# A four-layer transformer mix on one core: the feed-forward pipeline in a new order, and the recurrence's x terms as f16 hi/lo products

## The reference

```python
x = x + rnn(layernorm(x), cond, ctx)      # per sample and step:
#   logits = concat(x_t, h) @ W_attn.T + b_attn ;  aw = softmax(logits) ;  applied = aw @ enc
#   comb = relu(concat(x_t, applied) @ W_comb.T + b_comb)
#   h = tanh(comb @ W_ih.T + b_ih + h @ W_hh.T + b_hh) ;  out_t = h @ W_out.T + b_out
x = x + moe(layernorm(x))                 # 64 experts of width 64, router, one shared expert
x = x + attention_block(layernorm(x), cond, ctx)
#   self-attention, cross-attention (16 heads), then the gated feed-forward:
#   h3 = layernorm(y) * (1 + scale) + shift ;  u = h3 @ w1 + b1 ;  a, gate = split(u)
#   y = a * gelu(gate) @ w2 + b2 + y
x = x + layernorm(x) @ W_eff              # last layer, W_eff folds weight and disha
```

## Time and profile before

| | us |
|---|---|
| median of 3 runs | 1099.95 (1096.5 to 1100.71) |
| the profiled execution | 1102.3 |
| its span, first to last instruction | 1100.6 |

### The profile page before, as it was taken

One profiled execution on the slowest core, in us unless ns is written; L12 is line 12 of the kernel. 1 busy time (PEld: TensorE's weight loads), 2 busy tenths in 40 slices (PEclk: granted clock), 3 DMA queues, 4 the chain that ended last, 5 costly groups with the idle time before them and its releaser, 6 DMA issues. The chain is left out here.

```text
span 1100.6 us, 29712 instructions
## 1 busy us (share of the span) xinstructions
PE 960.0 (87%) x12346; PEld 644.8 (59%) x12346; DVE 721.7 (66%) x1778; ACT 478.0 (43%) x889; POOL 564.9 (51%) x519
## 2 busy tenths in 40 slices
PE   3698987699999999999979968889999999898765
PEld 2476766455555555555434426677777777776443
DVE  5545445557676766677776656778787878777543
ACT  2232223132232323332322216677777777778531
POOL 4688601033433334343645554666666676667663
PEclk9555555589999999999999988999999999999877
DMA  9120024232222222312334410000000000000000
GB/s 249 32 70 1 1 49 91 48 82 78 58 78 63 77 60 77 83 59 66 108 82 114 121 52 1 2 3 3 3 3 3 3 3 3 3 3 2 3 10 29
DMA packets 46202, 51.66 MB, mean 47 GB/s; under 512 B 22101, under 2 KB 36726, under 8 KB 46070
## 3 DMA queue, kind: packets, MB, share of 16 engines
q1 hardware_dynamic: 43152, 48.78, 17.1%
q10 hardware_dynamic: 2918, 1.01, 0.5%
HBM read 48.20 MB, written 1.57 MB: 45 GB/s over the span
## 5 line engine op out<-in xcount | busy, mean ns | idle before, releaser
L706 POOL TENSOR_TENSOR ex<-ex,xn 128x512 f32<-128x512 f32 x128 | 162.7, 1271 | 276.0 <-ACT thcb L941 152.6
L941 ACT ACTIVATE thcb<-ps 128x512 f32<-128x512 f32 x132 | 79.0, 599 | 214.7 <-PE ps L1735 213.7
L787 POOL TENSOR_TENSOR wu<-encC,wu 128x1024 f16<-128x1024 f32 x64 | 137.8, 2169 | 57.6 <-ACT encC L1009 57.6
L1742 PE MATMUL ps<-ex,wd 128*128 128x512 f32 x256 | 138.9, 625 | 0.5 <-DVE xT L1360 0.5
L1348 DVE SCALAR_TENSOR_TENSOR ex<-thcb,ps 128x512 f32<-128x512 f32 x132 | 90.5, 686 | 63.5 <-ACT thcb L941 60.9
L1735 PE MATMUL ps<-xnT,wg 128*128 128x512 f16 x384 | 106.7, 388 | 3.5 <-DVE ex L1354 3.5
L1735 PE MATMUL ps<-xnT,wu 128*128 128x512 f16 x384 | 106.5, 387 | 0.0
L1682 PEld LDWEIGHTS ps<-eb,encC 128*128 128x128 f16 x3072 | 86.8, 99 | 32.3 <-DVE eb L1220 19.3
L1791 PE MATMUL ps<-wg,M 128*128 128x128 f16 x1536 | 97.7, 221 | 2.1 <-DVE wg L1438 2.1
L781 POOL TENSOR_TENSOR wd<-wd,a_sum 128x512 f32<-128x512 f32 x64 | 66.6, 1044 | 63.3 <-DVE a_sum L1469 63.3
L1002 ACT CAST wu<-ps 128x1024 f16<-128x1024 f32 x64 | 64.9, 1014 | 73.6 <-PE ps L1826 73.6
(11 more groups left out here) (300 smaller groups left out, 1807.5 us busy)
## 6 DMA issues: line engine op xcount, KB each, us to landing
xn<-coef_rows SPq DMA_DIRECT2D x128, 256.0 KB, 3.9
thcb<-in_L_ffn_Wg SPq DMA_DIRECT2D x8, 256.0 KB, 4.1
thcb<-in_L_ffn_Wu SPq DMA_DIRECT2D x8, 256.0 KB, 3.4
wd<-in_L_ffn_Wd SPq DMA_DIRECT2D x2, 1024.0 KB, 10.3
xtok<-in_x SPq DMA_DIRECT2D x4, 256.0 KB, 6.1
thcb<-in_ctx SPq DMA_DIRECT2D x2, 512.0 KB, 11.4
wu<-in_L_xcond_attn_wq SPq DMA_DIRECT2D x2, 512.0 KB, 11.1
wu<-in_L_xcond_attn_wk SPq DMA_DIRECT2D x2, 512.0 KB, 10.7
```

Source lines behind the costliest of these rows:

```text
L706: nc.gpsimd.tensor_tensor(hid[:, side(m, n), :], gu[:, side(m, n), :], other, ALU.mult)\
L787: nc.gpsimd.tensor_tensor(z[:, 1, 8 * u:8 * u + 8, :], a_Zc[:, u], z[:, 0, 8 * u:8 * u + 8, :], ALU.subtract)\
L941: nc.scalar.activation(th[:, side(m, n), :], bank(side(m, n)), ACT.Tanh, scale=0.5 / WSCALE)\
L1742: mm(bank(5), wd[:, n, :] if n < PAIRS else swd[:, :], hid[:, side(m, n), :], start=(n == 0), stop=(n == UNITS - 1)).then_inc(s["y_ready"], 1)
```

## The change

**1. x terms and biases of the recurrence.** `x_parts` and the bias of `project` are made from f16 halves. A value is split into a high and a low f16 part; a product of two split values is three products (high by high, high by low, low by high), one of ones with a split row is two. `x_parts` is now 3 + 3 + 2 f16 products of 128 columns instead of three f32 ones; the bias of `project` two f16 products instead of one in f32. ACT makes the high parts of two weights, the bias rows and ones (four copies behind the first three groups of the set-up); DVE makes three low parts ahead of the low parts of the encoder; `xnT` is split as well, high parts by ACT and low parts by DVE, four groups of 512 columns behind the encoder's. PE waits for all of them before the first step.

```diff
 def x_parts(t):
-    xs, x_bank = xnT[:, t * B:(t + TL) * B], bank(X_BANK)
-    mm(x_bank[:, 0:TL * B], w_T[:, 0, :], xs, start=True, stop=False, skip_group_check=True)
-    mm(x_bank[:, LOGITS], xs, w_attnT[:, 0, :], start=False, stop=False, skip_group_check=True)
-    mm(x_bank[:, LOGITS], ones_row[:, :], battn_row[:, :], start=False, stop=False, skip_group_check=True)
+    if t == 0:
+        pe.wait_ge(s["wx_lo"], 3)
+    for i, (u, v) in enumerate(HALVES):
+        mm(x_bank[:, 0:TL * B], wx[:, 0, u, :], xs[v], start=(i == 0), stop=False, skip_group_check=True)
+    for u, v in HALVES:
+        mm(x_bank[:, LOGITS], xs[v], wx[:, 1, u, :], start=False, stop=False, skip_group_check=True)
+    for v in range(2):
+        mm(x_bank[:, LOGITS], ones16[:, :], rows16[:, v, 0:2 * L], start=False, stop=False, skip_group_check=True)
...
+dve.wait_ge(s["wx_hi"], 4)
+for i, w in enumerate((w_T, w_attnT)):
+    V.tensor_tensor(wx[:, i, 1, :], w[:, 0, :], wx[:, i, 0, :], sub).then_inc(s["wx_lo"], 1)
+V.tensor_tensor(rows16[:, 1, :], b_rows[:, :], rows16[:, 0, :], sub).then_inc(s["wx_lo"], 1)
```

```diff
 for n in range(ITEMS):                      # POOL
     Z_low(n, 0)
     Z_low(n, 1)
-    if n >= ITEMS - 2:
-        f_rstd1(n - (ITEMS - 2))
+    if n == ITEMS - 3:
+        f_rstd1(0)
...
     normalise(n, 0)
     normalise(n, 1)
...
+    if n == ITEMS - 2:
+        f_hi_lo(0)
+    if n == ITEMS - 1:
+        f_rstd1(1)
+    if n >= ITEMS - 4 and n < ITEMS - 1:
+        f_x3_sum(n - (ITEMS - 4))
```

```diff
 for u in range(FF + FF_LAG):                # PE
     k, c = divmod(u, FC)
-    if u < FF:
+    if 0 < u < FF:
         f_up(u)
-    if u == 0:
+    if u == 1:
         PT(ITEMS - 1, 0)
         PT(ITEMS - 1, 1)
-    elif u == 1:
+    if u >= FF_LAG:
+        f_down(u - FF_LAG)
+    if u == 2:
         O(ITEMS - 1, 0)
         O(ITEMS - 1, 1)
-    elif u == 2:
+    elif u == 3:
         pe.wait_ge(s["a_OT"], ITEMS)
         back(len(STAGES) - 1)
-    if u >= FF_LAG:
-        f_down(u - FF_LAG)
-    if c == 3 and k >= 1:
-        f_n2T_(k - 1)
-    if c == 0 and k + 1 < CH:
-        f_nT(k + 1)
+    if u + 1 in F_NT:                       # F_NT = {2: 1, 5: 2, 9: 3}
+        f_nT(F_NT[u + 1])
     if c == 0 and k >= 2:
+        f_n2T_(k - 2)
+    if c == 1 and k >= 2:
         f_last(k - 2)
...
 for u in range(FF + FF_LAG):                # POOL
     k, c = divmod(u, FC)
+    if c == 2 and 1 <= k < CH:
+        f_rstd2(k - 1)
     if u < FF:
         f_hid_low(u)
+    if u in F_NT:
+        f_hi_lo(F_NT[u])
     if c == 0 and k + 2 < CH:
         f_rstd1(k + 2)
-    if c == 2 and k >= 1:
-        f_rstd2(k - 1)
-    if c == 2 and k + 1 < CH:
-        f_hi_lo(k + 1)
-    if c == 3 and k < CH:
-        f_x3_sum(k)
+    if u == FC + 2:
+        f_x3_sum(CH - 1)
...
 for u in range(FF + FF_LAG):                # ACT
-    if c == 0 and k >= 2:
+    if c == 1 and k >= 2:
         f_n2T_in(k - 2)
...
     if u < FF:
         f_hid_hi(u)
-    if c == 2 and k + 1 < CH:
-        f_h_hi(k + 1)
+    if u == 0:
+        f_norm1(1)
+    if u in F_NT:
+        f_h_hi(F_NT[u])
     if c == 2 and k + 2 < CH:
         f_norm1(k + 2)
```

More of the change, by code:

```diff
@@ L239, in build @@
         f_hs = [xT_f[:, (2 + i) * CT:(3 + i) * CT].bitcast(F16).rearrange("p (x n) -> p x n", x=2) for i in range(2)]
-        f_x3 = [tiles(xnT[:, 1024 + i * CT:1024 + (i + 1) * CT]) for i in range(2)]
+        f_x3 = [tiles(ctxT[:, k * CT:(k + 1) * CT]) for k in range(CH)]
         f_split = [(w1[:, i * CT:(i + 1) * CT], [w1h[:, x, i * CT:(i + 1) * CT] for x in range(2)]) for i in range(2)]
@@ L256, in build @@
         LAST_BANK = 7
+        F_NT = {FC * (k - 1) + 1 if k > 1 else 2: k for k in range(1, CH)}
         def f_tok(t, k):
@@ L378, in build @@
             groups.append(("xn_ready", [(i * P, tr(xn[:, 4 * g + i, :])) for i in range(4)],
-                           xnT[:, g * 512:(g + 1) * 512], None))
+                           tuple(xnT[:, g * 512:(g + 1) * 512].bitcast(F16).rearrange("p (x a b) -> p x a b", x=2, b=P)[:, x]
+                                 for x in range(2)), None))
         N_RNN = len(groups)
@@ L893, in setup @@
                     evac(act, copy, g)
-            for g in range(N_RNN):
+            for g in range(3):
+                setup(g)
+            evacuated(act, 1)
+            for i, w in enumerate((w_T, w_attnT)):
+                copy(wx[:, i, 0, :], w[:, 0, :]).then_inc(s["wx_hi"], 1)
+            act.wait_ge(s["rnn_w_in"], 16 * RNN_DMAS)
+            act.wait_ge(s["consts_ready"], 2)
+            copy(rows16[:, 0, :], b_rows[:, :]).then_inc(s["wx_hi"], 1)
+            copy(ones16[:, :], ones_row[:, :]).then_inc(s["wx_hi"], 1)
+            for g in range(3, N_RNN):
                 setup(g)
@@ L1501, in f_stats1, with f_scale @@
                 f_stats(1, k, f_tok(a2tok, k), "f_stats1")
-            def f_modulate(k):
-                scale, shift = (ss[:, i, 8 * k:8 * k + 8].unsqueeze(2).broadcast_to([P, 8, T]) for i in (4, 5))
+            def f_scale(k):
+                scale = ss[:, 4, 8 * k:8 * k + 8].unsqueeze(2).broadcast_to([P, 8, T])
                 n8, h8 = (v.rearrange("p (b t) -> p b t", t=T) for v in (bank(nT_bank(k)), f_h32))
```

102 lines of the change are left out of this document (63 added, 39 removed).

## The result

The changed kernel takes **1084.65 us** (median of four runs, 1080.55 to 1087.7); the kernel before took 1098.86 (four runs, 1096.5 to 1100.71) in the same comparison. The ratio is 0.987, with a 95% interval of 0.983 to 0.991. So the change is a gain of 14 us, clear of the spread. But it is half of the 29 us forecast, and the time lies outside the range of 1063 to 1082: 13.7 us above the 1071 forecast.

What follows compares the result with a forecast made beforehand. PE was taken to bound the recurrence, with waits at the end. Profiled 1102.3 - 13.0 + 2.4 - 18.4 = 1073.3; the median lies 2.35 lower, so 1071 us, range 1063 to 1082.

Steps and rivals of the forecast that it cites:

- Part 1: Recurrence: x terms and biases as f16 products, set-up cost at the start included, 13.0 us less.
- I take the f16 rows, which have the same columns and the same type: `x_parts`: each of eight f16 products, one-row ones included, priced at 0.0625 us at the full clock.
- the upper bound of 0.17: `x_parts`: highest price of an f16 product at the full clock, 0.17 us, as one f32 instruction pays.
- the recurrence keeps half of its time: Rival: one-row products and loads cost more, 6.5 of 13 us stay, 1077.5 us; chance 0.10.
- Part 2: End of attention: first feed-forward chunk prepared inside stage 7, +2.4 us on the start of item 31.
- POOL has four operations, 6.4 us, in an item of about 10 us, so the `f_x3` sums ... in items 28 and 29 are covered by its idle time: Attention items 28 and 29: the sums, 2.6 us with the handover, fit into POOL's idle time.
- Part 3: From S of item 31 to the end, new order of the units: 72 us against 90.4, 18.4 less.
- the feed-forward gives back half: Rival: a 3.4 us wait lowers the clock, later waits grow, 9 of 18.4 us left, 1080; chance 0.20.
- walk: Feed-forward: the five engine lists followed in order from S of item 31, ending at 72 us.
- in the walk no DVE operation is held up by POOL: Feed-forward assumption: taken to cancel against up and down together 0.24 us longer than the undisturbed pace.
- POOL shuts out DVE: Rival, feed-forward: three shifts and three normalisings at their longest cost 6 us, 1077; chance 0.08.
- a clock that stays low: Rival, recurrence: low clock for longer, 2.6 us more per two-unit step, 1113 with 16 steps; chance 0.02.

Runs made afterwards that it cites:

- p1_only: The kernel before with only the f16 x terms and biases and their set-up, attention and feed-forward unchanged; 1092.6 us, ratio 0.9939.
- p23_only: The changed kernel with x terms, biases and their set-up back in f32, the attention and feed-forward changes kept; 1088.98 us, ratio 0.9919.
- x3_early: The changed kernel with POOL's `f_x3` sums of chunks 0 and 1 one item earlier, in items 27 and 28; 1077.33 us, ratio 0.9809.
- x3_at25: x3_early with the `f_x3` sum of chunk 0 in item 25 instead of 27; 1085.26 us in one execution.
- ff_clear: x3_early with POOL's `f_x3` sums of chunks 2 and 3 moved to units 3 and 8 of the feed-forward; 1073.67 us, ratio 0.9753.

## Why the prediction was wrong, and where it was right

**Part 1: right mechanism, two terms mis-sized.** The step that failed is "I take the f16 rows, which have the same columns and the same type". For the six products with 128 rows it was right (0.055 us, I had 0.0625). For the two with one row the upper bound of 0.17 came out, not as their price but as two changes of the number of rows, 0.09 us each, for which the sum had no term. At the full clock a step with x_parts became 0.39 us shorter and not 0.54, at the low one 0.77 and not 0.86, a step with the output bias 0.31 and not 0.4: 11.2 us in place of 13.75. The start cost 1.3 to 1.6 us, not 0.75, because the three differences on DVE took 1.6 us together (36.14 to 37.75) and not 0.8; the excess is the one that stood beside POOL. Net 10.1 us by the pair p1_only and p23_only. The rival "the recurrence keeps half of its time" had the one-row products as its place, at twice the size. The 9.7 of the profiled executions also hold a slower rise of the clock after the change (two steps of 10.77 and 9.55 us, in p1_only 10.76 and 7.05) and, before it, one step of 8.92 us that takes 7.24 elsewhere; the two nearly cancel.

**Part 2: the step that failed.** "POOL has four operations, 6.4 us, in an item of about 10 us, so the `f_x3` sums ... in items 28 and 29 are covered by its idle time". POOL's own time was covered. What was not is DVE: the normalise stood beside the sum and took 3.89 us instead of 1.72. x3_early shows that the rest of the estimate was exact (12.63 and 9.62), x3_at25 that the sum does the same anywhere. The 2.2 us on DVE became 5.8 on PE, since the wait went from 1.8 to 3.9 us and the clock was down behind it for Z, S and item 30. Of the 5.8, the 3.7 in item 29 come in all four traces with this order (3.5 to 3.7); the 2.0 in item 30 are in this trace alone, and so in part luck. I had the mechanism among the rivals, with the price of a normalise beside POOL, but I looked for it in the feed-forward and gave it 0.08; I had applied it where operations were moved on DVE, not where the change moved one on POOL.

**Between the parts.** +1.7 us between recurrence and item 28, where no instruction changed: low-clock pairs of items, 9 and 10 in the kernel before, 17 and 18 in the changed one, and a longer pair at 1 and 2. The prediction took no spread for this. It is not a part of the change, but it moves a single execution by 2 to 3 us.

**Part 3: mostly right.** Predicted 72 us from S of item 31, measured 73.9. The wait at the first transpose did leave the clock down, as the rival "the feed-forward gives back half" had it (up 2 took 2.77 us), but the waits behind it did not grow with it. Up 4 at 22.9 us (walk: 23.1), up 8 at 32.3 (32.9), up 12 at 47.4 (46.4), the last down until 60.8 (59.7), and 13.1 behind it (12.4). The 1 us at up 12 is again DVE beside POOL: the normalise of chunk 0 took 3.20 us beside `f_x3_sum(3)` and a low part, PE waited 2.7 instead of 1.4, and up 9 ran at the low clock. ff_clear gave this back. The assumption "in the walk no DVE operation is held up by POOL" was the wrong one.

Of the rivals, "POOL shuts out DVE" is the one that happened: 6 us by its own price, 5.8 in items 29 and 30, about 1 in the feed-forward and 0.9 at the start by the traces. That the sum came near its price is luck: it was made up for three shifts and three normalisings of the feed-forward. The one on the other side, a clock that stays low, did not come, and the change is faster, as forecast.

What stays open: why a wait of 2 us lowers the clock in one stage and not in the next, and why a change between 128 rows and one costs 0.09 us.

## What to carry to other kernels

When work is moved onto an engine's idle time, ask not only whether that engine has room but what the engine that shares its way to SBUF does then. An SBUF-to-SBUF normalise on DVE went from 1.1 us with POOL idle to 1.7, 3.9 and 5.6 beside it; on ACT it took 1.65, whether POOL was busy or not. A wait that is hidden behind another costs nothing until the first is removed, so an estimate from a list of waits has to be walked through in order, up to the engine that is busiest next.
